# Where SyncE waits for the residual in the preparation of a selective scan

## Chip, cores and metric

The kernel runs on one core of a Trainium2 chip (trn2). The metric is the time of one execution in microseconds (us) on the device. The engines that matter here are TensorE (PE), VectorE (DVE), ScalarE (ACT), GpSimd (POOL) and SyncE (SP). SyncE computes nothing: it waits on semaphores and issues DMA transfers, strictly in the order of its program.

## The reference, cut to what matters

A batch of 8 sequences of 1024 tokens with 256 channels passes through two mixture-of-experts layers around causal attention, two channel-mixing layers, and between those a state-space (Mamba) layer. Only the first part of that layer is touched by the change:

```python
mu = x.mean(-1, keepdims=True)
var = x.var(-1, keepdims=True)
h = (x - mu) / jnp.sqrt(var + EPS) * ln_gamma + ln_beta
xz = jnp.einsum('bld,ed->bel', h, in_proj_w)
u, z = jnp.split(xz, 2, axis=1)
uc = _silu(conv(u) + conv_b)              # depthwise, 4 taps, causal
x_dbl = jnp.einsum('bdl,ed->ble', uc, x_proj_w)
dt, Bm, Cm = jnp.split(x_dbl, [DT_RANK, DT_RANK + D_STATE], axis=-1)
delta = softplus(jnp.einsum('blr,dr->bdl', dt, dt_proj_w) + dt_proj_b)
```

Its x is itself the layer norm of the running sum. The recurrence then uses delta, delta times uc, Bm and Cm; its output plus uc times D is multiplied by silu(z), and the running sum is added back to the layer's projected output. That sum, with the normed x, is the "residual" below.

## The kernel before, in words

The kernel is a chain of stages, each a block of five engine programs ordered by semaphores alone, with a barrier between stages. The stage in question is `mamba_inputs` (L1752 to L2171). It walks over the 8 sequences (b = 0 to 7, `B` = 8). Per sequence the inner dimension of 512 is cut into 4 tiles of 128 channels (`IT_` = 4, index j), each 128 x 1024 in fp32.

For a sequence b the work is, in order of its data:

- SyncE loads x (`load(b)`, L1844) into one of three buffers `xt`. VectorE takes its statistics (`stat`, L2030; `gathered`, L2037). GpSimd turns them into scales by nine tiny instructions (`scales(b)`, L1903). VectorE then applies them twice: `normed(b)` (L2046) writes `xm`, what the projections read, and `residual(b)` (L2056) writes `xr`, the residual, of which there is **one** buffer. VectorE's `residual(b)` waits until the store of sequence b-1's residual has landed (`xr_stored`).
- TensorE transposes `xm` (L2128), ScalarE evacuates it (`turned`, L1939). TensorE projects the 4 tiles of u and the 4 of z ("the gates"). ScalarE does the first tap of the convolution (`tap_last`, L1946), VectorE the other three (`convolved`, L2064), ScalarE the silu of both (`silu_u`, `silu_z`).
- TensorE forms x_dbl (L2142), ScalarE copies it out (L1969), TensorE makes the deltas before their softplus (L2150), ScalarE and VectorE split the softplus into |v| (`absolute`, L1977), exp, log(1 + .) on one side and max(v, 0) on the other (`positive`, L2078).
- `deltas(b, j)` (L1830) adds the two parts into `dl` (L1835) and multiplies by uc into `du` (L1839). GpSimd does this for b = 0 to 6, VectorE for b = 7. There are only `NDU` = 3 buffers `du` for 4 tiles, so before it writes `du` of tile j = 3, GpSimd waits (L1838) until the store of the `du` of tile j = 0 of the same sequence has landed.
- SyncE stores all results to DRAM: residual, the gates' silu (`zsd`), uc (`ucd`), `dl` (`dd`), `du` (`dud`), and Bm with Cm (`bcd`).

The engines' programs are skewed over the sequences. The parts that count here are written out by hand:

- GpSimd's loop (L1930): for each b, first the four `deltas(b-1, j)`, then `scales(b+2)`.
- VectorE's loop (L2097): `positive(b)`, `normed(b+2)`, the four convolutions of b+1 with the statistics of a later sequence set in between, `gathered(b+3)`, `residual(b+2)`.
- ScalarE's loop (L1997): gates and silu of b, `turned(b+1, 0)`, `x_dbl(b)`, `turned(b+1, 1)`, absolute, exponential and logarithm of b, with the first taps of b+1 set in between.
- SyncE's loop (L1867): below, in the section on the change. Residuals 0 and 1 are stored ahead of it (L1865, L1866). SyncE's `residual(b)` (L1847) is one wait for VectorE's `xr` of b and one 1 MB store; its `deltas(b, j)` (L1851) is one wait for `du` of that tile and two stores of 512 KB.

Of the kernel before, what the change touches and what calls it, by code (L numbers as in the profile page):

```python
# [19 lines left out]
B, L, D = 8, 1024, 256  # L20
# [69 lines left out]
def rows(x, i):  # L90

    return x.rearrange("(b t p) d -> b p t d", t=LT, p=P)[i]
# [1659 lines left out]
def mamba_inputs(nc, tag, x_in, x_res, dd, dud, bcd, ucd, zsd, w, consts):  # L1752
# [5 lines left out]
    with ExitStack() as ctx:  # L1758
# [65 lines left out]
        def multiplied(b):  # L1824
            return du_ready if b < B - 1 else du_last

        def made(b, j):
            return IT_ * b + j + 1 if b < B - 1 else j + 1
# [12 lines left out]
        with nc.Block() as block:  # L1841
            @block.sync
            def _(sp):
                def load(b):  # L1844
                    sp.dma_start(xt[b % NX][:, :, :], rows(x_in, b)).then_inc(x_loaded[b % NX], 16)

                def residual(b):  # L1847
                    sp.wait_ge(xr_ready, b + 1)
                    sp.dma_start(rows(x_res, b), xr[:, :, :]).then_inc(xr_stored, 16)

                def deltas(b, j):  # L1851
                    n = IT_ * b + j
                    sp.wait_ge(multiplied(b), made(b, j))
                    sp.dma_start(dd[b][j * P:(j + 1) * P, :], dl[b % 2][j][:, :]).then_inc(dl_stored[b % 2], 16)
                    sp.dma_start(dud[b][j * P:(j + 1) * P, :], du[n % NDU][:, :]).then_inc(du_stored[n % NDU], 16)

                load(0)
                for dst, src in ((ident[:, :], consts["ident"]), (vec[:, :], w["vec"]),
                                 (w_in[:, :, :], w["w_in"].rearrange("(h p) e -> p h e", p=P))):
                    sp.dma_start(dst, src).then_inc(consts_loaded, 16)  # L1860
                load(1)
                for dst, src in ((w_x[:, :, :], w["w_x"].rearrange("(h p) e -> p h e", p=P)), (w_dt[:, :], w["w_dt"])):
                    sp.dma_start(dst, src).then_inc(consts_loaded, 16)
                load(2)
                residual(0)  # L1865
                residual(1)  # L1866
                for b in range(B):  # L1867
                    if b + NX < B:
                        sp.wait_ge(xr_ready, b + 1)
                        sp.wait_ge(xm_ready, b + 1)  # L1870
                        load(b + NX)
                    for j in range(IT_):
                        if b and j:
                            deltas(b - 1, j - 1)
                        sp.wait_ge(zs_ready, IT_ * b + j + 1)
                        sp.dma_start(zsd[b][j * P:(j + 1) * P, :], zs[j][:, :]).then_inc(zs_stored[j], 16)
                    sp.wait_ge(uc_ready, IT_ * (b + 1))
                    sp.dma_start(ucd.rearrange("b (j p) t -> b p j t", p=P)[b], uc[b % 2][:, :, :]).then_inc(uc_stored[b % 2], 16)
                    if b:
                        deltas(b - 1, IT_ - 1)  # L1880
                    sp.wait_ge(xd_ready, 2 * b + 2)
                    for c, lo in ((0, DTR), (BANK, 0)):
                        sp.dma_start(bcd[b][:, c:c + BANK], xd[lo:lo + 2 * NS, c:c + BANK]).then_inc(xd_stored, 16)
                    if b + 2 < B:
                        residual(b + 2)
                for j in range(IT_):
                    deltas(B - 1, j)
                sp.wait_ge(xr_stored, 16 * B)
                sp.wait_ge(xd_stored, 32 * B)
                for j in range(IT_):  # L1890
                    sp.wait_ge(zs_stored[j], 16 * B)
                for u in range(2):
                    sp.wait_ge(uc_stored[u], 16 * (B // 2))
                    sp.wait_ge(dl_stored[u], 16 * IT_ * (B // 2))
                for u in range(NDU):
                    sp.wait_ge(du_stored[u], 16 * len(range(u, IT_ * B, NDU)))
# [1046 lines left out]
```

## Time and profile before

| | us |
|---|---|
| median of 3 runs | 4733.85 (4733.12 to 4746.62) |
| the profiled execution, own time | 4738.97 |
| its span | 4737.2 |
| busy in the span: PE / DVE / ACT / POOL | 4081.9 / 3092.8 / 2332.1 / 2379.9 |
| the stage `mamba_inputs`, about 2615 to 3067 in the span | 452 |
| the scan behind it, about 3067 to 4360 | 1293 |

The profile is of one execution. "PE" is TensorE's matrix multiplies, "PEld" its loads of weights. "Idle before" an instruction is the time in which its engine stood still, and the name behind the arrow is what ended that. "SPq" and "DMA" rows are issues and transfers. The three characters after a time in a timeline row give the engine; merged rows say how many instructions they hold (x8).

In the sections below, "turn b" means the start of ScalarE's evacuation `turned(b, 0)`, once per sequence. These starts are at 2668.99 (b = 1), 2709.77 (2), 2770.32 (3), 2831.20 (4), 2892.33 (5), 2950.81 (6) and 2991.19 us (7). They cut the stage into one period per sequence.

### The profile page before, as it was taken

What the parts mean: (1) busy time and instruction counts of PE and PEld (TensorE: products, weight loads), DVE (VectorE), ACT (ScalarE), POOL (GpSimd) and SP (SyncE); (2) the same over time, 40 slices, a digit from 0 to 9 for tenths busy, and PEclk for the clock granted to TensorE, in tenths of its full rate; (3) what the DMA queues carried; (4) which work ended last, traced back from release to release, by engine and by line L of the source; (5) the groups of instructions that cost most, each with busy time, mean ns of one, the idle gap of its engine ahead of it and who ended that gap; (6) DMA issues with size and microseconds to landing.
All of it is one profiled execution on the core that took longest, in us unless ns stands there. A gap on an engine that the chain in (4) does not pass through costs nothing. (4 is left out here: it accounts for less than half of the span.)

```text
span 4737.2 us, 119303 instructions
## 1 busy us (share of the span) xinstructions
PE 4081.9 (86%) x49836; PEld 2639.8 (56%) x49836; DVE 3092.8 (65%) x5297; ACT 2332.1 (49%) x3872; POOL 2379.9 (50%) x1558
## 2 busy tenths in 40 slices
PE   6399788899999998389969767799999999997698
PEld 6266554233333327356657333378788878876576
DVE  5411154888888867611155566589899899997575
ACT  1022133577777771111234455677767776774233
POOL 1134444222222224034422234489999999998464
PEclk6599998899999998599989888899999999999899
DMA  6133366656566527143331444744334343332662
GB/s 221 60 74 51 65 223 212 91 92 96 95 95 96 98 62 247 31 115 51 45 95 56 149 170 181 263 105 102 98 90 100 98 102 84 101 101 81 240 231 71
DMA packets 339597, 549.39 MB, mean 116 GB/s; under 512 B 55488, under 2 KB 239200, under 8 KB 339040
## 3 DMA queue, kind: packets, MB, share of 16 engines
q1 hardware_dynamic: 285552, 467.46, 37.5%
q0 software_dynamic: 24576, 34.10, 4.5%
q10 hardware_dynamic: 28912, 40.02, 2.4%
q8 instruction: 397, 6.50, 0.6%
q14 instruction: 160, 1.31, 0.1%
HBM read 327.30 MB, written 212.32 MB: 114 GB/s over the span
## 5 line engine op out<-in xcount | busy, mean ns | idle before, releaser
L2489 POOL TENSOR_TENSOR s_hc<-s_hs,s_ct 128x1024 f32<-128x1024 f32 x512 | 1214.2, 2386 | 71.7 <-DVE s_hs L2468 57.1
L2468 DVE TENSOR_TENSOR_SCAN s_hs<-s_dA,s_psB 128x1024 f32<-128x1024 f32 x512 | 1168.2, 2286 | 105.2 <-PE s_psB L2395 32.3
L2395 PE MATMUL s_psB<-s_diag,s_duT 128*32 128x128 f32 x32768 | 974.1, 275 | 74.3 <-DVE s_hs L2468 41.8
L2395 PEld LDWEIGHTS s_psB<-s_diag,s_duT 128*32 128x32 f32 x32768 | 919.0, 111 | 177.7 <-issue 92.2
L1351 DVE CUSTOM_DVE_ANT_0 a_masked<-a_psM,k_later 128x1024 f32<-128x1024 f32 (+7 forms) x1024 | 724.8, 750 | 145.3 <-PE a_psM L1409 142.5
L1333 ACT ACTIVATE a_wt<-a_psE 128x512 f32<-128x512 f32 (+1 forms) x1216 | 625.2, 579 | 268.0 <-PE a_psE L1435 258.2
L2339 ACT ACTIVATE s_dA<-s_dlt,s_aneg 128x1024 f32<-128x1024 f32 x512 | 587.5, 1147 | 342.2 <-DVE s_hs L2468 338.6
L1312 POOL TENSOR_SCALAR_AFFINE_SELECT a_wt<-a_wt 128x512 f32<-128x512 f32 x256 | 163.2, 637 | 692.0 <-ACT a_wt L1333 691.9
L2319 ACT ACTIVATE s_diag<-s_ident,s_bt 128x128 f32<-128x128 f32 x972 | 322.1, 387 | 13.4 <-ACT s_ys L2328 13.4
L1409 PE MATMUL a_psM<-a_kst,a_qst 96*128 96x512 bf16 (+3 forms) x1152 | 305.7, 330 | 14.6 <-DVE a_mx L1351 10.8
L1435 PE MATMUL a_psE<-a_qst,a_kst 99*128 99x512 bf16 (+3 forms) x1152 | 308.6, 329 | 6.6 <-ACT a_wt L1333 6.4
L2138 PE MATMUL s_ps<-s_hT,s_w_in 128*128 128x512 f32 x512 | 235.6, 621 | 70.2 <-DVE s_cv L2074 69.0
L2408 PE MATMUL s_psY<-s_hc,s_gsum 128*32 128x512 f32 x2064 | 257.5, 598 | 5.9 <-POOL s_hc L2489 5.9
L1451 PE MATMUL a_psO<-a_wt,a_va 128*32 128x512 f32 (+3 forms) x2304 | 246.3, 499 | 0.4 <-POOL a_wt L1312 0.4
L1435 PEld LDWEIGHTS a_psE<-a_qst,a_kst 99*128 99x128 bf16 x1152 | 94.6, 97 | 249.5 <-ACT a_wt L1333 189.6
L2138 PEld LDWEIGHTS s_ps<-s_hT,s_w_in 128*128 128x128 f32 x512 | 100.8, 199 | 204.3 <-issue 123.2
L698 POOL DMA_INDIRECT x<-m1f_y,m_slots x64 | 100.9, 1576 | 175.3 <-DVE m1f_y L754 160.7
L698 POOL DMA_INDIRECT x<-m2f_y,m_slots x64 | 100.9, 1576 | 173.9 <-DVE m2f_y L754 159.2
L718 ACT ACTIVATE m1f_mid<-m1f_psU,m1f_bu 128x512 f32<-128x512 f32 x80 | 55.0, 687 | 237.5 <-PE m1f_psU L787 237.5
L718 ACT ACTIVATE m2f_mid<-m2f_psU,m2f_bu 128x512 f32<-128x512 f32 x80 | 54.9, 687 | 236.5 <-PE m2f_psU L787 236.4
L1409 PEld LDWEIGHTS a_psM<-a_kst,a_qst 96*128 96x128 bf16 x1152 | 105.4, 98 | 113.0 <-DVE a_mx L1351 59.8
L1839 POOL TENSOR_TENSOR s_du<-s_dl,s_uc 128x1024 f32<-128x1024 f32 x28 | 66.0, 2356 | 166.3 <-DMA dud<-s_du 164.6
(361 smaller groups left out, 6500.7 us busy)
## 6 DMA issues: line engine op xcount, KB each, us to landing
s_dlt<-dd SPq DMA_DIRECT2D x128, 512.0 KB
a_qst<-qs SPq DMA_DIRECT2D x144, 128.0 KB
a_kst<-ks SPq DMA_DIRECT2D x144, 128.0 KB
yd<-s_ys ACTq DMA_DIRECT2D x33, 512.0 KB
vs<-a_va ACTq DMA_DIRECT2D x32, 512.0 KB, 3.7
zsd<-s_zs SPq DMA_DIRECT2D x32, 512.0 KB, 8.7
ucd<-s_uc SPq DMA_DIRECT2D x8, 2048.0 KB, 14.2
dd<-s_dl SPq DMA_DIRECT2D x32, 512.0 KB, 9.2
```

Source lines behind the costliest of these rows:

```text
L1333: act.activation(wt[k % NW][:, x:x + c, 0:q1 - q0], psE[s % NE][:, 0:c * (q1 - q0)].rearrange("p (x q) -> p x q", x=c), ACT.Exp, scale=HD ...
L1351: dve.tensor_tensor_reduce(masked[u % 2][:, 0:w], psM[:, place[u]:place[u] + w], later[:, L - w:], 1.0, -3e38, ALU.add, ALU.max, mx[g % 2] ...
L1409: ins = pe.matmul(psM[:, place[u] + c:place[u] + c + r], qst[g % HG][0:SK, x, j * P:(j + 1) * P], kst[g % HG][0:SK, x, c:c + r], start=Tru ...
L1435: ins = pe.matmul(psE[s % NE][:, x * (q1 - q0):(x + 1) * (q1 - q0)], kst[g % HG][0:SK + PARTS, x0 + x, kt * P:(kt + 1) * P], qst[g % HG][0 ...
L1451: ins = pe.matmul(psO[AUG * x:AUG * (x + 1), q0 % BANK:q0 % BANK + q1 - q0], va[g % HG][:, kt, x, :], wt[k % NW][:, x, 0:q1 - q0], start=( ...
L2138: ins = pe.matmul(dst[:, c:c + BANK], w_in[:, h, e * P:(e + 1) * P], hT[b % 2][:, h, c:c + BANK], start=(h == 0), stop=(h == DH - 1))
L2319: ins = act.activation(diag[:, place(n, u), c, :], ident[:, :], ACT.Copy, scale=bt[u][:, c, n:n + 1])
L2339: act.activation(dA[k % 2][:, :], dlt[j % 2][:, q % NB, :], ACT.Exp, scale=aneg[:, k:k + 1]).then_inc(dA_ready, 1)
L2395: ins = pe.matmul(psB[s][DG * m:DG * (m + 1), c * P:(c + 1) * P], duT[j % 2][:, c, DG * r:DG * (r + 1)], diag[:, place(NB * g + m, u), c, ...
L2408: ins = pe.matmul(psY[DG * r:DG * (r + 1), c:c + BANK], gsum[:, :], hc[NB * (g % 2) + r][:, c:c + BANK], start=(g == 0), stop=(g == NQ - 1))
L2468: dve.tensor_tensor_scan(hs[k % 2][:, :], dA[k % 2][:, :], psB[s][:, :], 0.0, ALU.mult, ALU.add).then_inc(scanned, 1)
L2489: pool.tensor_tensor(hc[NB * (g % 2) + r][:, :], hs[k % 2][:, :], ct[:, g, :], ALU.mult).then_inc(weighed, 1)
```

## The change

SyncE's wait for the residual of sequence b+2 and its store stood last in round b of SyncE's loop, in front of everything of round b+1. Now the same wait and store stand in round b+1, behind the gates of sequence b+1 (its four `zsd` stores) and the first three deltas of sequence b, and ahead of `ucd`, the last deltas and `bcd` of that round. Nothing else differs: the same 8 residuals are stored, in the same order, and no engine's arithmetic is touched.

```diff
@@ -1874,6 +1874,8 @@
                             deltas(b - 1, j - 1)
                         sp.wait_ge(zs_ready, IT_ * b + j + 1)
                         sp.dma_start(zsd[b][j * P:(j + 1) * P, :], zs[j][:, :]).then_inc(zs_stored[j], 16)
+                    if 1 <= b < B - 1:
+                        residual(b + 1)
                     sp.wait_ge(uc_ready, IT_ * (b + 1))
                     sp.dma_start(ucd.rearrange("b (j p) t -> b p j t", p=P)[b], uc[b % 2][:, :, :]).then_inc(uc_stored[b % 2], 16)
                     if b:
@@ -1881,8 +1883,6 @@
                     sp.wait_ge(xd_ready, 2 * b + 2)
                     for c, lo in ((0, DTR), (BANK, 0)):
                         sp.dma_start(bcd[b][:, c:c + BANK], xd[lo:lo + 2 * NS, c:c + BANK]).then_inc(xd_stored, 16)
-                    if b + 2 < B:
-                        residual(b + 2)
                 for j in range(IT_):
                     deltas(B - 1, j)
                 sp.wait_ge(xr_stored, 16 * B)
```

## Rows read from the trace of the kernel before

**Rows 1.** Busy time and granted clock of two stretches: this stage, the scan.

```profile
core 0: us, PE busy (x) PEld busy (x) DVE busy (x) ACT busy (x) POOL busy (x), PEclk, DMA share, GB/s
...
2615.00:3067.00 452.00, 335.82 (x896) 152.39 (x896) 288.85 (x392) 253.51 (x248) 170.15 (x129) 0.87 0.51 192
3067.00:4360.00 1293.00, 1205.98 (x35152) 1024.27 (x35152) 1178.47 (x564) 924.55 (x1559) 1221.07 (x520) 0.98 0.38 95
```

**Rows 2.** The same view for six periods, cut at turns 1 to 7.

```profile
2668.99:2709.77 40.78, 40.41 (x114) 18.53 (x113) 26.49 (x45) 31.41 (x33) 19.71 (x15) 1.00 0.18 68
2709.77:2770.32 60.55, 42.06 (x112) 18.90 (x111) 42.35 (x50) 31.75 (x33) 23.55 (x17) 0.86 0.47 176
2770.32:2831.20 60.88, 42.96 (x113) 19.30 (x112) 42.01 (x49) 31.74 (x32) 23.65 (x17) 0.83 0.46 175
2831.20:2892.33 61.13, 43.28 (x113) 19.36 (x112) 42.14 (x49) 31.75 (x32) 23.58 (x17) 0.83 0.46 174
2892.33:2950.81 58.48, 42.82 (x113) 19.21 (x112) 40.00 (x49) 31.75 (x32) 23.74 (x17) 0.85 0.48 182
2950.81:2991.19 40.38, 40.01 (x113) 18.35 (x112) 25.90 (x33) 31.55 (x33) 23.59 (x17) 1.00 0.61 237
```

**Rows 3.** Waits, 2709 to 2951: us in total, times, longest.

```profile
POOL s_du L1839 <- DMA dud<-s_du: 124.6, 4, 36.3
...
PE s_ps L2138 <- DVE s_cv L2074: 68.4, 4, 18.1
...
DVE s_xm L2052 <- POOL s_r L1926: 26.9, 4, 7.3
```

**Rows 4.** Timeline of VectorE behind turn 3: start, duration.

```profile
2768.53 2.64 DVE L2060 TENSOR_SCALAR s_xr<-s_xt,s_one_r,s_mr 128x256 f32<-128x256 f32 x8
2780.65 4.86 DVE L2082 TENSOR_SCALAR s_pos<-s_ps,s_vec 128x1024 f32<-128x1024 f32 x4 [9.47 <-ACT s_dl L1982]
2792.19 17.07 DVE L2052 TENSOR_SCALAR s_xm<-s_xt,s_mv,s_r 128x256 f32<-128x256 f32 x8 [6.68 <-POOL s_r L1926]
```

**Rows 5.** Timeline of GpSimd in the same stretch.

```profile
2746.06 2.39 POOL L1835 TENSOR_TENSOR s_dl<-s_pos,s_dl 128x1024 f32<-128x1024 f32 x1
2784.42 2.36 POOL L1839 TENSOR_TENSOR s_du<-s_dl,s_uc 128x1024 f32<-128x1024 f32 x1 [35.98 <-DMA dud<-s_du]
...
2792.37 2.43 POOL L1835 TENSOR_TENSOR s_dl<-s_pos,s_dl 128x1024 f32<-128x1024 f32 x1 [0.22 <-ACT s_dl L1990]
```

**Rows 6.** Timeline of SyncE's issues in the same stretch.

```profile
2771.20 0.39 SPq L1849 DMA_DIRECT2D res<-s_xr  x1
...
2774.74 0.59 SPq L1855 DMA_DIRECT2D dud<-s_du  x1
```

**Rows 7.** SyncE's longest wait in this stage, whole span: us in total, times, longest.

```profile
SPq L1849 <- DVE s_xr L2060: 244.2, 8, 42.1
```

**Rows 8.** Timeline of VectorE, period 6.

```profile
2967.98 2.67 DVE L2052 TENSOR_SCALAR s_xm<-s_xt,s_mv,s_r 128x256 f32<-128x256 f32 x8 [1.98 <-POOL s_r L1926]
...
2988.80 3.17 DVE L2060 TENSOR_SCALAR s_xr<-s_xt,s_one_r,s_mr 128x256 f32<-128x256 f32 x8
```

**Rows 9.** Timeline of GpSimd, period 1.

```profile
2691.07 2.37 POOL L1835 TENSOR_TENSOR s_dl<-s_pos,s_dl 128x1024 f32<-128x1024 f32 x1 [18.40 <-ACT s_dl L1990]
...
2705.38 2.37 POOL L1835 TENSOR_TENSOR s_dl<-s_pos,s_dl 128x1024 f32<-128x1024 f32 x1
```

**Rows 10.** Timeline of ScalarE, period 1: the first and the last gate.

```profile
2696.23 1.02 ACT L1967 ACTIVATE s_zs<-s_ps 128x1024 f32<-128x1024 f32 x1
...
2708.86 1.01 ACT L1967 ACTIVATE s_zs<-s_ps 128x1024 f32<-128x1024 f32 x1
```

**Rows 11.** DMA, 2709 to 2771: GB/s in 40 slices; issues, median us to landing.

```profile
GB/s 0 42 329 244 266 302 365 420 420 420 420 420 418 418 423 423 423 420 412 279 1 0 0 0 0 0 0 0 0 0 0 0 11 0 0 0 0 0 0 0
DMA packets 4435, 10.66 MB, mean 172 GB/s; under 512 B 272, under 2 KB 2320, under 8 KB 4432
...
dud<-s_du SPq DMA_DIRECT2D x4, 512.0 KB, 12.0
```

## The prediction, made before the changed kernel ran

> **What bounds the kernel now.** I went from the stage table to the periods, then to the waits, and then to three timelines of one period. The stage takes 452 us and no engine fills it: TensorE, the busiest, works 336 us [rows 1]. Cut at the turns it falls into two kinds of period [rows 2]. Periods 1 and 6 take 40.78 and 40.38 us, with TensorE busy for nearly all of that. The four between take 60.55, 60.88, 61.13 and 58.48 us for the same instructions. So the question is what four sequences wait 20 us each for.
>
> The waits of those four periods name a loop [rows 3]: GpSimd waits 124.6 us for the landing of a store of du, VectorE waits 26.9 us for GpSimd's scales, TensorE waits 68.4 us for VectorE's convolutions. The timelines put it in order, for the period behind turn 3 (2770.32):
>
> 1. VectorE makes the residual at 2768.53 to 2771.17 [rows 4]. SyncE has stood at its wait for it (244.2 us in all eight waits, up to 42.1 in one) [rows 7]. It issues the residual's store at 2771.20 and only then the rest of the next round; the du of tile 0 goes out at 2774.74 [rows 6].
> 2. GpSimd finished its last dl at 2748.45. The du of tile 3 needs the buffer of tile 0, so it starts only at 2784.42, after 35.98 us of waiting. That is 9.7 us behind the issue at 2774.74. It ends at 2786.78; the scales stand behind it in GpSimd's program [rows 5].
> 3. VectorE ended its last s_pos at 2785.51 and waits 6.68 us for the scales. Then its eight s_xm take 17.07 us [rows 4], while GpSimd does seven instructions of about 2.4 us on the next deltas, begun at 2792.37 [rows 5]. The same eight take 2.67 us in period 6 [rows 8]. The excess is 14.4 us.
> 4. The convolutions stand behind s_xm in VectorE's program, and TensorE's next projections need the banks that they release.
>
> 6.68 and 14.4 are 21 us, the length by which such a period is too long. The row shows eight short instructions stretched to the length of seven GpSimd ones, about one per instruction. The Trainium skill (SBUF — State Buffer, "SBUF: two separate sides") says that VectorE in a two-port mode and GpSimd take a shared pair of SBUF ports as an exclusive lock for a whole instruction. By that rule the trace's 17.07 us is what one expects; shared bandwidth would give less.
>
> **The change, part by part.**
>
> *Removed: the wait ahead of the next round.* SyncE comes to the load of round b as soon as bcd of round b-1 is out. In period 1 the first gate is ready 28.3 us behind the turn (2697.25 against 2668.99) [rows 10]. GpSimd begins the deltas at +22.1 and its last dl ends at 2707.75, +38.8 [rows 9]; du of tile 0 is done at about +27 (two instructions). So its stores can be issued at about +30. The queue then holds three transfers of 512 KB; at the 420 GB/s of the burst [rows 11] they need 3.7 us. With the 9.7 us of step 2, which stood behind more data, it lands at +34 to +40, against +38.8 when it is needed. I take no wait, at most 1 us. GpSimd's last du then runs from +38.8 to +41.2, that is to 0.4 us behind the next turn, in place of 16.5 us behind it (2786.78 against 2770.32).
>
> *Scales.* They take 5.4 us (2786.78 to 2792.19) [rows 4, 5] and need VectorE's statistics, which are gathered just ahead of the residual. They end at about +6, with contention at +9. VectorE wants them when s_pos ends, at +15.2 (2785.51). The wait of 6.4 to 7.3 us goes, with 6 us or more to spare.
>
> *s_xm.* It runs from +15.2 to +17.9. GpSimd's next deltas need the first logarithm, at +22.1, so it is idle in between. The 14.4 us go as well. What is late next is ScalarE's row of taps and silus, just as in period 1, which is this pattern with the same statistics in between.
>
> *Added: the residual behind the gates.* SyncE reaches it when the last gate is made, 2709.87, just at the turn [rows 10]. xr is made at about +0.9 (2771.17), so the wait is about 1 us. Behind it stand ucd, the last deltas and bcd; bcd's data is ready only some 8 us behind the turn, and nobody needs these stores before ScalarE's x_dbl of the next period, 40 us on. They cost nothing. The store's own reader, VectorE's next residual, is also a period away. Issuing costs SyncE 0.4 to 1.3 us for each of the 15 transfers, under 20 us of a 40 us period.
>
> *Moved past: the load.* It is issued some 30 us earlier and has all the more time. The data is the same 10.66 MB per period; at 420 GB/s it needs 25 us of 40.8. Period 6 already moved 237 GB/s in 40.38 us without loss [rows 2]. So I cost the queues at nothing; if this cover failed, the wait would show up at GpSimd's last du.
>
> *New collision.* GpSimd's last du and the scales now fall on VectorE's eight xr (2.64 us). Period 6 shows one such overlap at its mildest: 3.17 us in place of 2.64 [rows 8]. The other bound is that xr waits until +0.4 and then alternates with nine scale instructions: 0.4 + 2.6 + 5.4, so it ends at +8.4. VectorE idles 9.47 us behind it until +10.3 [rows 4]. Between the ends I take the later one as possible; either way the cost is 0, with 2 us to spare.
>
> **Sum.** The four periods take 60.55 + 60.88 + 61.13 + 58.48 = 241.04 us. At the length of period 1 they take 4 x 40.78 = 163.12. The gain is **77.9 us**. By parts it would be 26.9 of waits and about 4 x 14 of stretching, 83; some 5 of that come back as the taps' waits that period 1 has and the long ones hide. The last two sequences were not held up and keep their length; there the store queue is less full, worth 0 to 1.5 us. The profiled execution took 4738.97 us, so 4661.1 is expected from it. It lies 5.1 us above the median of 4733.85; I put the forecast against the median: **4655.9 us**.
>
> **Rivals.**
>
> *A: the collision moves to the residual.* If GpSimd's deltas ran some 10 us later than I place them, because the store of the first du lands late behind other stores, xr would meet large instructions as s_xm did and take 17 us: from -1.4 to +15.7, 5.4 us past the start of s_pos. Four periods would give 22 us back: 4677. For it speaks that landings under load take a median of 12.0 us [rows 11]; against it that the queue is empty at that moment. By the skill's lock rule named above each of the eight can lose up to a whole GpSimd instruction, which is this case. It hangs on when GpSimd is busy; the rule does not say that. Chance 0.06.
>
> *B: the loop is cut, but half returns.* If the scales still came late by a landing behind the gates (SyncE now waits for each gate by turns), s_xm would start near +19 and meet the deltas from +22.1 only in part. About half of the gain goes: 4695. It needs the first du to land 13 us later than I work out. Chance 0.04.
>
> *C: no gain.* The change would do nothing if what held SyncE were not this wait. But SyncE issues everything within 1 us of the residual, in a burst [rows 6]. Chance 0.02.
>
> *D: slower.* The clock. The long periods have a granted clock of 0.83 to 0.86, the short ones 1.00 [rows 2], so some TensorE rest is lost ahead of the scan, in which it is busy 1206 of 1293 us at 0.98 [rows 1]. If the scan's clock fell in return, it would have to eat 78 us and 14 more: 92 of 1293 is 7%, a clock of about 0.91 or less if TensorE is what the scan waits for all the time. That gives 4750. Against it: period 6 and what follows hold 1.00 without a break, and VectorE and GpSimd are as busy as TensorE in the scan. Chance 0.02.
>
> **Numbers.** The forecast has 0.86. About 0.3%, 14 us, is what a measurement of this kernel can tell from no change. The forecast, A and B are all faster by more: 0.96; C is the same: 0.02; D is slower: 0.02. The bounds of the unknown terms are small: 3 us below (the emptier queue, periods of 40.38), up to 4 above for a late landing in each period. The runs before scatter by 13 us, upward. So the range is 4648 to 4671; it leaves out A, B, C and D, 0.14 in all.
>
> **What would show it.** The residual's store should be issued 0 to 9 us behind the turn and no longer be the wait that SyncE spends 30 to 40 us in; GpSimd's wait for dud should go from 124.6 us to under 10; VectorE's wait for the scales should vanish and all s_xm groups take 2.7 us; all six periods should take 40 to 41.5 us at a clock of 1.00. A group of s_xm or xr that takes 10 us or more would say A or B. Long periods with a short wait for dud would refute the loop, and a scan longer than 1300 us would say D.

## The result

| | before | changed |
|---|---|---|
| median, us | 4737.16 (4 runs, 4733.12 to 4746.62) | 4654.61 (4 runs, 4650.30 to 4663.69) |
| profiled execution, own time | 4738.97 | 4652.00 |
| its span | 4737.2 | 4650.1 |
| the stage, first load to first load of the next | 452.1 | 372.1 |

The ratio of the runs is 0.9825, 95% interval 0.9803 to 0.9848: 1.75% faster. The forecast, made against the median of 4733.85 known then, was 4655.9, the range 4648 to 4671.

First the six periods between turns 1 and 7, cut at the new turns, and under them the whole stage. The columns are those of [rows 2]: length; busy time and count of TensorE, its weight loads, VectorE, ScalarE, GpSimd; granted clock; DMA share; GB/s.

```profile
2663.69:2704.46 40.77, 40.40 (x114) 18.52 (x113) 26.48 (x41) 31.39 (x32) 21.63 (x16) 1.00 0.53 199
2704.46:2744.87 40.41, 40.04 (x113) 18.36 (x112) 29.32 (x49) 31.40 (x32) 23.70 (x18) 1.00 0.72 263
2744.87:2785.28 40.41, 40.04 (x113) 18.36 (x112) 29.31 (x49) 31.40 (x33) 23.70 (x18) 1.00 0.71 263
2785.28:2825.68 40.40, 40.03 (x113) 18.36 (x112) 29.30 (x49) 31.39 (x32) 23.69 (x18) 1.00 0.71 263
2825.68:2866.09 40.41, 40.03 (x113) 18.36 (x112) 29.31 (x49) 31.40 (x32) 23.69 (x18) 1.00 0.62 238
2866.09:2906.11 40.02, 39.65 (x112) 18.19 (x111) 27.81 (x34) 31.52 (x32) 23.28 (x18) 1.00 0.61 236
2610.00:2982.00 372.00, 324.57 (x896) 148.98 (x896) 243.61 (x392) 252.04 (x248) 170.44 (x129) 0.94 0.63 234
```

The four long periods of [rows 2], 241.04 us together, now take 161.63: 79.4 us gone. TensorE is busy for all but 0.4 us of each, at a clock of 1.00, so it is what bounds them now. Seen from TensorE the 79.4 us are two terms. Of the 241.04 us it waited 68.4 for VectorE's convolutions [rows 3], and it was busy for 171.1 where the same work now takes 160.1, 11.0 us more, while its granted clock (the mean over the period, 1.00 being full speed) was 0.83 to 0.86 [rows 2]. VectorE's busy time fell from 42 to 29 us per period without an instruction fewer, which is the stretching of its xm that has gone, less 1.6 us that xr now takes longer. The whole stage is 80.0 us shorter (2615.11 to 3067.20 before, 2610.03 to 2982.16 after). The two profiled executions differ by 87 us; the other 7 lie in stages that the change does not touch (5.1 ahead, 2.1 behind), as much as single runs of one kernel scatter.

The timeline of GpSimd around turn 3 (2744.87), start and duration, answers to [rows 5]:

```profile
2740.47 2.37 POOL L1835 TENSOR_TENSOR s_dl<-s_pos,s_dl 128x1024 f32<-128x1024 f32 x1
2742.92 2.36 POOL L1839 TENSOR_TENSOR s_du<-s_dl,s_uc 128x1024 f32<-128x1024 f32 x1
2745.36 0.24 POOL L1912 TENSOR_SCALAR s_veps<-s_mv 128x8 f32<-128x8 f32 x1
...
2750.55 0.20 POOL L1926 TENSOR_TENSOR s_r<-s_r 128x8 f32<-128x8 f32 x1
2766.58 2.37 POOL L1835 TENSOR_TENSOR s_dl<-s_pos,s_dl 128x1024 f32<-128x1024 f32 x1 [15.83 <-ACT s_dl L1990]
```

and that of VectorE to [rows 4]:

```profile
2743.43 4.26 DVE L2060 TENSOR_SCALAR s_xr<-s_xt,s_one_r,s_mr 128x256 f32<-128x256 f32 x8
2754.85 4.86 DVE L2082 TENSOR_SCALAR s_pos<-s_ps,s_vec 128x1024 f32<-128x1024 f32 x4 [7.16 <-ACT s_dl L1982]
2759.63 2.66 DVE L2052 TENSOR_SCALAR s_xm<-s_xt,s_mv,s_r 128x256 f32<-128x256 f32 x8
```

The last du follows its dl at once, the scales end 5.9 us behind the turn, and the eight xm run 14.8 to 17.4 us behind it, while GpSimd waits for the first logarithm until 21.7. The wait that took up SyncE's time is now that for the gates (first row); the residual's, 244.2 us before [rows 7], is 40.8 for the eight, of which about 27 belong to the two ahead of the loop:

```profile
SPq L1876 <- ACT s_zs L1967: 198.5, 32, 19.1
...
SPq L1849 <- DVE s_xr L2060: 40.8, 8, 13.6
```

### The profile page after: what moved, and what is told of

It is laid out like the page before. It is cut to its first block and busy times, and to the rows that moved or that the text cites. A ratio compares the mean times of both kernels' runs of the same rounds, so it can differ in the third digit from the quotient of the medians.

```text
span 4650.1 us, 119303 instructions
## 1 busy us (share of the span) xinstructions
PE 4060.0 (87%) x49836; PEld 2623.5 (56%) x49836; DVE 3047.3 (66%) x5297; ACT 2330.4 (50%) x3872; POOL 2378.7 (51%) x1558
## 5 line engine op out<-in xcount | busy, mean ns | idle before, releaser
L2319 ACT ACTIVATE s_diag<-s_ident,s_bt 128x128 f32<-128x128 f32 x972 | 322.2, 388 | 13.4 <-ACT s_ys L2328 13.4
L2138 PE MATMUL s_ps<-s_hT,s_w_in 128*128 128x512 f32 x512 | 224.2, 598 | 1.7 <-ACT s_hT L1943 1.3
L787 PE MATMUL m1f_psU<-m1f_gT,m1f_wup 128*128 128x512 f32 x320 | 141.7, 598 | 1.7 <-DVE m1f_gT L743 0.9
```

The costliest lines, as they stand in the source:

```text
L2138: ins = pe.matmul(dst[:, c:c + BANK], w_in[:, h, e * P:(e + 1) * P], hT[b % 2][:, h, c:c + BANK], start=(h == 0), stop=(h == DH - 1))
L2319: ins = act.activation(diag[:, place(n, u), c, :], ident[:, :], ACT.Copy, scale=bt[u][:, c, n:n + 1])
```

## The experiments

Ten kernels ran beside the kernel before. Since stages elsewhere scatter by several us from run to run, the table at the end also gives the length from turn 1 to turn 7 (322.2 us before, 242.4 changed). In four further kernels that keep the gain (four du, scales first, residual behind the first tile, GpSimd held before tile 2) it is 242.4 to 242.5.

### The wait alone, put back

The changed kernel with this at the end of each round of SyncE's loop:

```diff
+                    if b + 2 < B:
+                        sp.wait_ge(xr_ready, b + 3)
```

> The changed kernel with one more instruction: SyncE waits for the next residual at the end of each round again, but the residual's store stays where the change put it. Theory (the wait is what counts, because it holds back the store of the first du): the long periods are back, four of 58 to 61 us, GpSimd waits 25 to 36 us per period for the landing of dud, time 4730 to 4745. Rival 1 (the order of the 1 MB store, or the load brought forward, made the gain): the gain stays, 4650 to 4665.

Measured: 4664.58 us, ratio to before 0.9835 (0.9810 to 0.9859). The gain stayed, against the theory. SyncE stands at the residual again, but the four periods take 41.5 to 41.9 us, not 60. The timeline of GpSimd behind turn 3 (2752.64) of this kernel:

```profile
2763.69 2.36 POOL L1839 TENSOR_TENSOR s_du<-s_dl,s_uc 128x1024 f32<-128x1024 f32 x1 [14.57 <-DMA dud<-s_du]
...
2771.22 0.20 POOL L1928 TENSOR_TENSOR s_r<-s_r 128x8 f32<-128x8 f32 x1
2774.70 2.37 POOL L1835 TENSOR_TENSOR s_dl<-s_pos,s_dl 128x1024 f32<-128x1024 f32 x1 [3.29 <-ACT s_dl L1992]
```

and of VectorE and SyncE:

```profile
2771.46 2.67 DVE L2054 TENSOR_SCALAR s_xm<-s_xt,s_mv,s_r 128x256 f32<-128x256 f32 x8 [3.63 <-POOL s_r L1928]
```

```profile
2753.53 0.39 SPq L1845 DMA_DIRECT2D s_xt<-x  x1
2753.96 0.58 SPq L1876 DMA_DIRECT2D zsd<-s_zs  x1
2754.59 0.43 SPq L1854 DMA_DIRECT2D dd<-s_dl  x1
2755.06 0.91 SPq L1855 DMA_DIRECT2D dud<-s_du  x1
```

SyncE's wait holds up everything behind it, and then a burst of transfers goes out at once. Here too the first du goes out in that burst, only behind the turn, and GpSimd waits 14.6 us for it to land. But without the residual's 1 MB in front GpSimd goes on 3 us earlier, 10.2 us behind the start of the burst in place of 13.2. The scales end 18.8 us behind the turn in place of 21.9. The eight xm end at 2774.13, and GpSimd's next large instruction begins at 2774.70: they slip through a gap with 0.6 us to spare. So there is a **threshold** that I had not seen: the wait costs about 1 us a period; being 3 us later still costs 19.

### Four buffers for du

The kernel before with SyncE's order untouched:

```diff
-        NX, NCV, NPS, NDU = 3, 3, 4, 3
+        NX, NCV, NPS, NDU = 3, 3, 4, 4
```

> The kernel before, SyncE's order untouched, but with four buffers for du in place of three, so that GpSimd does not need the landing of the first du of a sequence to write its fourth. Theory (a loop from SyncE's wait over the third buffer to the scales): the loop is cut here as well, although SyncE still stands 30 us and more at the residual; periods 40 to 42 us, time 4650 to 4665. Rival 1 (SyncE's lateness itself costs: gates, uc and deltas stored in a late burst): little or nothing is gained, 4720 to 4740.

Measured: 4657.30 us, ratio 0.9819 (0.9793 to 0.9844); periods of 40.42 us. As the theory said: the loop is cut at another link, and the gain is the same, while SyncE still stands at the residual.

```profile
SPq L1849 <- DVE s_xr L2060: 147.2, 6, 34.9
```

(SyncE's longest wait in 2700 to 2990 of this kernel.) Its lateness by itself costs nothing.

### The scales ahead of the last deltas

The kernel before; in GpSimd's loop:

```diff
-                        for j in range(IT_):
+                        for j in range(IT_ - 1):
                             deltas(pool, b - 1, j)
                     if b + 2 < B:
                         scales(b + 2)
+                    if b:
+                        deltas(pool, b - 1, IT_ - 1)
```

> The kernel before, but GpSimd computes the scales ahead of the deltas of tile 3 instead of behind them; GpSimd still waits as long for the landing of dud. Theory (the late du costs only because the scales stand behind it in GpSimd's program): VectorE no longer waits for the scales, its eight xm take 3 to 5 us, periods 40.5 to 43, time 4655 to 4670. Rival (the late du is needed by itself, by the stores or by the next deltas): at least half of the 20 us per period stays, 4690 or more.

Measured: 4660.91 us, ratio 0.9828 (0.9803 to 0.9853); periods of 40.43 us. The late du is harmless as soon as the scales do not stand behind it. It still stretches one xm: the du that starts at 2720.85 in the timeline of GpSimd meets the eight xm of 2721.41 in that of VectorE, which take 4.2 us in place of 2.7.

```profile
2720.85 2.37 POOL L1839 TENSOR_TENSOR s_du<-s_dl,s_uc 128x1024 f32<-128x1024 f32 x1 [7.53 <-DMA dud<-s_du]
```

```profile
2721.41 4.21 DVE L2054 TENSOR_SCALAR s_xm<-s_xt,s_mv,s_r 128x256 f32<-128x256 f32 x8
```

### GpSimd held until xm is done

The kernel before; in GpSimd's loop, ahead of the deltas:

```diff
+                        if b + 1 < B:
+                            pool.wait_ge(xm_ready, b + 2)
```

> The kernel before, but GpSimd begins a sequence's deltas only when VectorE has finished the xm beside them. The wait for the late scales stays, 6.4 to 7.3 us in each of four periods; the eight xm run beside an idle GpSimd. Theory (two separate terms, the wait and the stretching by GpSimd's instructions): the xm take 2.7 us in place of 15 to 17, a period takes 46 to 47 us, the gain is about 4 x 14 = 56 us, time 4678 to 4690. Rival (the xm are long for another reason, their data or the stores): they stay at 15 us or more, and the time at 4735 or above.

Measured: 4682.58 us, ratio 0.9882 (0.9859 to 0.9905); periods of 46.92, 45.42, 46.63 and 45.28 us. This measures the stretching apart: without it the scales, as late as before, make a period 4.9 to 6.5 us longer than 40.4, and the other 14 go (56.8 us over the four). The 4.9 to 6.5 are not all waiting. TensorE's clock has a part in them. First the period behind turn 3 of this kernel, then TensorE's wait in it, then the same period of the kernel with the wait alone, where the clock is 1.00:

```profile
2752.53:2797.95 45.42, 41.96 (x113) 18.85 (x112) 27.62 (x49) 31.74 (x32) 23.55 (x17) 0.96 0.62 234
```

```profile
PE s_ps L2140 <- DVE s_cv L2076: 3.1, 1, 3.1
```

```profile
2752.64:2794.17 41.53, 40.54 (x113) 18.19 (x112) 27.71 (x49) 31.45 (x33) 23.60 (x17) 1.00 0.66 256
```

Of the 5.0 us by which 45.42 exceeds 40.41, 3.1 are a wait for the convolutions and 1.9 a longer busy time of TensorE (41.96 against 40.04). A row of VectorE's timeline, behind turn 4 (2797.95):

```profile
2819.59 2.67 DVE L2054 TENSOR_SCALAR s_xm<-s_xt,s_mv,s_r 128x256 f32<-128x256 f32 x8 [6.45 <-POOL s_r L1926]
```

The wait for the scales is about what it was, 6.68 us in [rows 4], the duration is 2.67 us in place of 17. Nothing but GpSimd's concurrent instructions made xm long.

### The residual behind the first tile alone

The changed kernel with the residual's wait and store moved forward once more:

```diff
                         sp.wait_ge(zs_ready, IT_ * b + j + 1)
+                        if j == 1 and 1 <= b < B - 1:
+                            residual(b + 1)
                         sp.dma_start(zsd[b][j * P:(j + 1) * P, :], zs[j][:, :]).then_inc(zs_stored[j], 16)
-                    if 1 <= b < B - 1:
-                        residual(b + 1)
```

> The changed kernel, but the residual's wait and store stand behind the first tile's deltas alone, ahead of the stores of gates 1 to 3 and of the deltas of tiles 1 and 2, so that SyncE stands there some 10 us in every period and stores the rest late. Theory (only the store of the first du has to go out ahead of the wait): the whole gain stays, periods 40 to 41.5 us, 4648 to 4662. Rival (all gates and deltas have to be ahead of it): 5 to 20 us per period come back, 4675 or more.

Measured: 4661.24 us, ratio 0.9842 (0.9821 to 0.9863); turn 1 to 7 in 242.43 us, the same as the changed kernel to 0.01 us. SyncE waits up to 13.7 us for the residual in a round, and nothing comes of it. It is enough that the first tile's stores go out ahead of the wait.

### The collision moved to the residual, twice

The changed kernel, GpSimd held before tile k = 2, and in a second kernel k = 1:

```diff
                         for j in range(IT_):
+                            if j == k:
+                                pool.wait_ge(cv_ready, IT_ * (b + 1))
                             deltas(pool, b - 1, j)
```

> The changed kernel, but GpSimd begins the deltas of tile 2 only when VectorE has finished the convolutions of the sequence, some 2 us ahead of the turn, so that four large GpSimd instructions meet the eight xr. Theory (VectorE has 7 us or more to spare behind the residual, and GpSimd 4 or more ahead of the xm): the xr take 9 to 12 us, the start of s_pos and the periods stay, 4648 to 4662. Rival (there is no such slack): one to five us per period are lost, 4662 to 4680.

Measured: 4657.85 us, ratio 0.9828 (0.9807 to 0.9849). The eight xr take 10.62 us, and the periods 40.40: the slack behind the residual is real and hides 8 us.

> The same with the deltas of tiles 1, 2 and 3 held, six large instructions: the collision that rival A of the prediction named, moved to the residual. Theory: the xr take 14 to 17 us and end behind the point where s_pos could start, the scales end at about +17 behind the turn and VectorE waits for them; 4 to 7 us per period are lost in five periods, 4675 to 4695. Rival (slack is larger than worked out): up to 2 us per period, 4655 to 4665.

Measured: 4687.17 us, ratio 0.9894 (0.9874 to 0.9915). VectorE's and GpSimd's rows around turn 2 (2698.67), in one timeline:

```profile
2696.84 2.37 POOL L1835 TENSOR_TENSOR s_dl<-s_pos,s_dl 128x1024 f32<-128x1024 f32 x1 [12.06 <-DVE s_cv L2076]
...
2697.23 14.77 DVE L2062 TENSOR_SCALAR s_xr<-s_xt,s_one_r,s_mr 128x256 f32<-128x256 f32 x8
...
2708.86 2.35 POOL L1839 TENSOR_TENSOR s_du<-s_dl,s_uc 128x1024 f32<-128x1024 f32 x1
...
2711.92 4.85 DVE L2084 TENSOR_SCALAR s_pos<-s_ps,s_vec 128x1024 f32<-128x1024 f32 x4
```

This is the mechanism of rival A, priced. Beside six large instructions xr ends 13.3 us behind the turn. s_pos follows at once, 3 us later than it could, and the five periods behind take 44.4 to 44.8 us: 4.0 to 4.4 lost in each, the low edge of what was expected. VectorE did not wait for the scales, which ended at 2716.56, some 0.2 us ahead of the end of s_pos; that part of the expectation was wrong.

### The threshold

The first experiment had left open why the kernel before is so much slower than the kernel with the wait alone. New theory: the bytes ahead of the first du in SyncE's queue, whatever they carry, decide whether the xm end before the first logarithm lets GpSimd go. Three kernels put it to the test. Two start from the kernel with the wait alone and store one or two more gates ahead of the first deltas, for b of 1 to 6. The first has `first` = 2 there, as shown, the second 3:

```diff
-                    for j in range(IT_):
-                        if b and j:
-                            deltas(b - 1, j - 1)
+                    first = 2 if 1 <= b < B - 1 else 1
+                    for j in range(IT_):
                         sp.wait_ge(zs_ready, IT_ * b + j + 1)
                         sp.dma_start(zsd[b][j * P:(j + 1) * P, :], zs[j][:, :]).then_inc(zs_stored[j], 16)
+                        if b and first - 1 <= j < IT_ - 1:
+                            deltas(b - 1, j - first + 1)
+                    for j in range(IT_ - first, IT_ - 1):
+                        if b:
+                            deltas(b - 1, j)
```

> The kernel with the wait alone put back, and in its burst one more transfer of 512 KB (the store of gate 1) issued ahead of the first deltas. Theory now (a threshold: the wait hardly costs by itself; what counts is when the first du has landed, which the bytes ahead of it in the queue set, since every xm that has not run when the first logarithm comes, 22 us behind the turn, is stretched to 2.4 us): the first du lands 1.3 to 1.6 us later, the scales end at +20, one to three of the eight xm are stretched, periods of 44 to 49 us in place of 41.5, time 4672 to 4695. Rival (what counts is the residual's store alone, in front): nothing changes, periods 41.5 to 42.5, 4656 to 4672.

Measured: 4691.90 us, ratio 0.9887 (0.9862 to 0.9913); periods of 53.37, 48.38, 46.93 and 45.71 us. The first lies above the 44 to 49 expected (its eight xm took 10.97 us); the time is inside.

> The same with two more transfers of 512 KB (gates 1 and 2) ahead of the first deltas: as many bytes ahead of the first du as in the kernel before, but with the residual's store behind. Theory: the scales end at +21 to +22, five to eight of the xm are stretched, periods of 53 to 61 us, time 4710 to 4740: the kernel before is back without the residual in front. Rival: periods 41.5 to 43, 4656 to 4675.

Measured: 4726.02 us, ratio 0.9966 (0.9952 to 0.9980); periods of 60.47, 55.23, 54.97 and 57.65 us. As expected, most of the loss is back with the residual's store behind: 67 of the 80 us between turns 1 and 7. The last du starts 12.6 us behind the burst's first issue, in the kernel before 13.2. So the same 3 MB are not quite worth the same whatever they carry; what makes the 0.6 us was not tested.

The third starts from the kernel before, with the residual where it was, and moves only the load:

```diff
-                    if b + NX < B:
-                        sp.wait_ge(xr_ready, b + 1)
-                        sp.wait_ge(xm_ready, b + 1)
-                        load(b + NX)
+                    def load_next():
+                        if b + NX < B:
+                            sp.wait_ge(xr_ready, b + 1)
+                            sp.wait_ge(xm_ready, b + 1)
+                            load(b + NX)
+                    if b == 0:
+                        load_next()
                     for j in range(IT_):
                         if b and j:
                             deltas(b - 1, j - 1)
+                            if j == 1:
+                                load_next()
```

> The kernel before, with the residual's wait and store in front of the round as they were, and only the load of a later sequence, 1 MB, moved from behind the residual to behind the first tile's deltas. Theory: 1 MB fewer ahead of the first du, so it lands 2.5 to 3 us earlier, the eight xm end just before GpSimd's next deltas, periods 41 to 43 us, time 4655 to 4672, nearly the whole gain of the change with the residual unmoved. Rival (the residual in front is what costs): periods stay at 58 to 61, 4730 or more.

Measured: 4664.94 us, ratio 0.9839 (0.9814 to 0.9864); periods of 41.08 to 41.45 us. The residual in front, wait and store, costs next to nothing when the load is not in front too.

The timelines of VectorE give the eight xm behind turn 3; first the kernel with one more gate ahead (turn 3 at 2761.36), then with two (2765.35), then with the load behind (2750.71):

```profile
2781.53 6.83 DVE L2058 TENSOR_SCALAR s_xm<-s_xt,s_mv,s_r 128x256 f32<-128x256 f32 x8 [4.98 <-POOL s_r L1932]
```

```profile
2786.59 12.97 DVE L2058 TENSOR_SCALAR s_xm<-s_xt,s_mv,s_r 128x256 f32<-128x256 f32 x8 [6.05 <-POOL s_r L1932]
```

```profile
2769.07 2.67 DVE L2057 TENSOR_SCALAR s_xm<-s_xt,s_mv,s_r 128x256 f32<-128x256 f32 x8 [3.17 <-POOL s_r L1931]
```

With the others, in the order of the start of xm. "Ahead" is what SyncE issues in the burst before the first du (its dl included); "to du" the time from the burst's first issue to the start of GpSimd's last du; start and length of the eight xm, and the period, are those of turn 3; all in us:

| kernel | ahead | to du | xm starts, behind the turn | xm take | period | turn 1 to 7 |
|---|---|---|---|---|---|---|
| changed | not late | | 14.8 | 2.7 | 40.4 | 242.4 |
| before, load behind | 2 MB | 9.7 | 18.4 | 2.7 | 41.1 | 246.0 |
| wait alone | 2 MB | 10.2 | 18.8 | 2.7 | 41.5 | 247.7 |
| one more gate | 2.5 MB | 11.5 | 20.2 | 6.8 | 48.4 | 275.5 |
| two more gates | 3 MB | 12.6 | 21.2 | 13.0 | 55.2 | 309.5 |
| before | 3 MB | 13.2 | 21.9 | 17.1 | 60.9 | 322.2 |
| GpSimd held until xm is done | 3 MB | 13.2 | 21.8 | 2.7 | 45.4 | 265.4 |

In all the late ones, but for the held one, GpSimd's next deltas begin 22.05 or 22.06 us behind the turn. Up to 18.8 a later start is nearly free; from there 3.1 us cost 19.4 us, six for one. The last row shows that 15.5 of the 19.4 go with the stretching: as late a start without it gives a period of 45.4, against 60.9 with it and 41.5 with the wait alone. TensorE's lower clock is inside both parts: its busy time in this period is 40.5 us with the wait alone, 42.0 held and 43.0 before, and the rest of its period is idle time, 1.0, 3.5 and 17.9 us.

## Why the prediction was right

The sum went by a measured period of the same work, and the steps can be checked one by one. *The periods*: 40.41 us in place of the 40.78 taken from period 1, which gives 79.4 in place of 77.9. *The first gate* goes out 28.3 us behind the turn (2691.98 against 2663.69), as worked out; the last du of GpSimd ends 0.4 us behind the next turn (2745.28 against 2744.87), as worked out, and GpSimd has no wait for a landing left in these periods (124.6 us in four before). *The scales* end at 5.9 us, forecast 6 to 9. *xm* starts at 14.8, forecast 15.2, and takes 2.66. *The collision* with xr costs 1.6 us of the slack, between the two bounds; 7.2 of 9.5 us of idle time are left ahead of s_pos. *The residual's store* goes out 2.9 us behind the turn (2747.72), and neither ucd nor bcd behind it holds anyone up. The clock is 1.00 in all six periods, and the scan did not pay for it (1668 us from its first load to the end of the span, 1670 before; a granted clock of 0.99 over its first 1293 us, 0.98 before), which leaves nothing of rival D. Rival A did not occur; where it was brought about with six large instructions, it cost 4.0 to 4.4 us a period, against the 5.4 of the prediction, which had xr take 17 us and not 14.8.

What the prediction had too simply was step 1 of its list, the cause of the loop's length. It named SyncE's wait for the residual, and took the excess for a fixed 21 us: 6.7 of wait and 14.4 of stretching. The runs show that the wait is not enough. Of the 20 us per period the wait without those bytes is worth 1.1 to 1.5; the rest came from 1 MB, 3 us of queue, in front of the first du, which pushed the xm past the first logarithm. That the bytes need the wait in turn is argued and not shown: every kernel with 2.5 MB or more ahead had the wait too. The prediction also called the 1 MB load "moved past" without a price; in front of the first du it was worth as much as the residual's own store. Here the forecast was lucky: the change removes the wait as well as the bytes.

Two further terms were wrong without harm. The agreement of 6.68 + 14.4 = 21 with the excess is partly chance. It leaves out two things of opposite sign: part of the lateness was slack, since a start of xm at 18.8 costs next to nothing, and TensorE's lower clock added 2.0 to 3.2 us of busy time to each long period, a term that the prediction priced only for the scan. The period taken as the yardstick had a clock of 1.00, so the sum contained it. And rival B was priced far too high: it has a start of xm near +19 give back half of the gain, while the kernel with the wait alone starts there and gives back 5.3 of the 80 us.

Two readings were inexact. SyncE issues 17 transfers in a full round and not 15; at 0.4 to 1.3 us each that is still at most some 22 us of 40. Rival C has SyncE issue everything within 1 us of the residual; the burst starts 0.03 us behind it, but its first du goes out 3.6 us behind (2774.74 against 2771.17).

What makes the other stages differ by some us from run to run was not followed up. A second residual buffer was not tried.

## What to carry to other kernels

When a wait in a store queue costs far more than its length, look for what the late transfer releases two steps on, and for what runs beside it there; the price may jump once some work no longer fits its gap, so measure how far it is from that point before you price the wait. In a program of stores, put first the one that gives back a buffer somebody waits for, and behind it whatever nobody waits for, loads for a distant round included. Before a VectorE instruction that slows down beside GpSimd, ask in which gap it falls: here one more buffer, a new order in GpSimd's program and several in SyncE's each brought the gain or nearly all of it, because each kept eight short instructions within the gap.

## What the hardware showed beside this

The stretching is not a property of every GpSimd instruction. In the changed kernel the eight xr around turn 2 (2704.46) overlap the last du and then the first scales, among them a power over 128 x 8 that takes 1.73 us. First the xr within 2703.0 to 2704.8 (count, then ns minimum, median and maximum, then first and last start), then those within 2705.3 to 2707.0 with the ones on either side, then the power in GpSimd's timeline:

```profile
L2060 DVE TENSOR_SCALAR s_xr<-s_xt,s_one_r,s_mr x1: 1996/1996/1996, 2703.0 to 2703.0; 128x256 f32<-128x256 f32 x1
```

```profile
L2060 DVE TENSOR_SCALAR s_xr<-s_xt,s_one_r,s_mr x7: 400/402/404, 2704.9 to 2706.9; 128x256 f32<-128x256 f32 x7
```

```profile
2705.28 1.73 POOL L1914 TENSOR_TENSOR s_r<-s_veps,s_neg_half 128x8 f32<-128x8 f32 x1
```

The one beside the du of 128 x 1024 took 2.0 us, until that had ended. The seven behind it took 0.40 us each, one every 0.33 us, as they do beside an idle GpSimd (2.64 to 2.67 us for eight), and by their even spacing five of them started inside the power. This goes by the profile's times for GpSimd, which are rough. The Trainium skill (SBUF — State Buffer, "SBUF: two separate sides") has the shared ports locked for a whole instruction; for the large ones every trace here agrees, one VectorE instruction let through per GpSimd instruction, and for this one it does not: the long time of a small power blocks none of the five. The prediction's bound, by which xr alternates with the scales' 5.4 us, was too high for that reason.
